# A decoder kernel whose constants and loads of x become pieces of the planned block

## The chip, the cores and the metric

The kernel runs on 1 core of a Trainium2 chip. The metric is the device time of one execution in microseconds. The chip has five engines with queues of their own: TensorE (PE, matrix products; PEld is its loading of weights), VectorE (DVE), ScalarE (ACT), GpSimd (POOL) and SyncE (SP, which here issues nearly all DMAs). Engines wait for each other through semaphores.

## The reference, cut to what matters

Two decoder layers over x, 2 sequences of 1024 rows of 256 numbers. Layer 0 is causal self attention, cross attention over 77 context rows and a mixture of 8 linear experts. Layer 1 has a recurrence over the 1024 positions in the place of self attention, then cross attention and a gated mixture of 16 experts beside a shared one.

```python
x = x + _L0_attn_ref(_layernorm(x, axis=-1), L0_attn_w_qkv, L0_attn_w_proj)
x = x + _L0_xattn_ref(_layernorm(x, axis=-1), ctx_768, mask_BxS2_bf1, L0_xattn_Wq, L0_xattn_Wk, L0_xattn_Wv, L0_xattn_Wo)
x = x + _L0_ffn_ref(_layernorm(x, axis=-1), L0_ffn_Wg, L0_ffn_bg, L0_ffn_We, L0_ffn_be)
x = x + _L1_attn_ref(_layernorm(x, axis=-1), L1_attn_Wi, L1_attn_bi, L1_attn_Wh, L1_attn_bh)
x = x + _L1_xattn_ref(_layernorm(x, axis=-1), ctx_768, L1_xattn_wq, ..., L1_xattn_bo)
x = x + _L1_ffn_ref(_layernorm(x, axis=-1), L1_ffn_router_w, ..., L1_ffn_shared_down_w)
```

The recurrence (`_L1_attn_ref`) is h(t) = tanh(Wi x(t) + bi + Wh h(t-1) + bh). Step t needs step t-1, so its 1024 steps run one after the other.

## The kernel before, in words

The rows are cut into 4 chunks of 512 (256 of each sequence, 4 tiles of 128). Every operation of every layer and chunk is a *piece*: a small function that waits on semaphores and issues a few instructions. A stage's pieces are all put into one block. `st.add(engine, name, function, count, cost, rank, after, ...)` registers a kind of piece: its engine, how many there are, an assumed cost in us, a rank (the lower one goes first) and how long after its end its signal is assumed to be seen. `Plan.make` then walks through time with these assumed numbers. At each turn it takes, over all engines, the piece that could begin earliest, and among equals the one of lowest rank; a piece can begin once the semaphores that it waits for are reached, which `Rehearsal` finds out by running the piece's function on a recorder. The outcome is a fixed order of pieces on each engine. So a shift of a few tenths of a microsecond at the start can change which piece goes first at any later place.

Between two steps of the recurrence the planner fits other pieces where it expects room. Where it expects PE to pause for over 0.1 us it puts in idle matmuls (L536, class `Recurrence`), whose result nobody reads.

The names that matter below:

- `tanh` (L562, L563) and `sub` (L568) with the products L519: the recurrence's step on ACT, DVE and PE.
- `ChunkNorm`: statistics (L435, L437, L440, DVE), `power` (L446, POOL, reads `neg_half`), `normalise` (L453, DVE), `turn` (L460, PE, transposes with `ident`); it serves all six layer norms.
- L764 with L776 and L787: queries and keys of the self attention of a chunk, rounded, and kept in two parts; they go to the DRAM tensors `q_scr`, `k_scr` and come back into `heads` by DMA.
- L968/L971 and L977: scores, mask (`mask_qk`, `identb`) and their row maxima; L1026/L1029 scores the other way round (`mask_kq`); L1040 the exponential; L1055 the product with the values.
- L749, L1251, L1263, L1294, L1305, L1319: the same for cross attention; `x_qs` is loaded by DMA from `qx_scr`.
- L1459/L1485: the experts of layer 0. L1687/L1755: gate and up, and down products of layer 1's gated experts, the last work of a chunk; `cT` (L1658) and `spread` (L1716, reads `sel_pair`) belong to it.
- `fill` (L2067, L2070): memsets of `heads`, 10 large ones before the first scores.
- `load` (L1925 to L1942): the loads of ctx, mask and weights of layer 0.

Before all that, `constants` runs a block of its own: SP issues the 8 loads of x and the one of wqkv, DVE sets eight constants, POOL waits for all eight and shapes seven of them, and the block's end is a barrier for all engines. The planned block comes behind it, and the planner is told by `given` that x and wqkv are there at time 1.0.

## Time and profile before

| | |
|---|---|
| median of 3 runs | 1354.29 us (1351.82 to 1355.94) |
| the profiled execution's own time | 1351.89 us |
| its span in the profile | 1350.2 us |
| mean granted clock of TensorE | 0.97 of full speed |
| PE busy | 1291.7 us, 96% |
| DVE busy | 857.6 us, 64% |
| ACT busy | 628.5 us, 47% |
| POOL busy | 38.7 us, 3% |

Busy shares are means over stages with different limits, and PE's includes the idle matmuls. A view by stretches of time and the waits in each tell more than the page's first lines.

### The profile page before, as it was taken

The numbers are of one execution on the slowest core, as the hardware profiler recorded it, in microseconds if no ns is written. First come the engines' busy times: TensorE is split into PE (matmuls) and PEld (weight loads), VectorE is DVE, ScalarE is ACT, GpSimd is POOL, SyncE is SP. The second block draws the span as 40 slices with busy tenths as digits, with TensorE's granted clock in tenths as the row PEclk, the third lists the DMA queues.
The fourth block names the chain that finished last, engine by engine and source line by source line (L and its number), as shares of the span: only waits on it lengthen the run. The fifth ranks groups of instructions, "written<-read, shape, count | busy, mean of one in ns | idle before, by whom it ended". The sixth has DMA issues, their size and how long they took to land.

```text
span 1350.2 us, 48630 instructions
## 1 busy us (share of the span) xinstructions
PE 1291.7 (96%) x19707; PEld 897.4 (66%) x19707; DVE 857.6 (64%) x2733; ACT 628.5 (47%) x2842; POOL 38.7 (3%) x60
## 2 busy tenths in 40 slices
PE   4598899999999999999999999999999999999998
PEld 2464446777766777776677777776767677766555
DVE  5875398258688326877762255677656575567586
ACT  2162403753533784443457865633544345442422
POOL 1010000000000000000000000000000000000000
PEclk9798779999999999999999998999999799999999
DMA  5536300001000000100000014010000100001000
GB/s 167 133 99 164 83 1 3 15 15 50 3 3 2 15 9 20 60 6 3 3 3 27 3 45 147 5 50 3 2 3 18 42 11 3 2 18 48 2 17 16
DMA packets 50753, 44.48 MB, mean 33 GB/s; under 512 B 10667, under 2 KB 49766, under 8 KB 50534
## 3 DMA queue, kind: packets, MB, share of 16 engines
q1 hardware_dynamic: 48934, 40.59, 10.2%
q8 instruction: 160, 2.62, 0.8%
q10 hardware_dynamic: 1600, 0.79, 0.3%
q14 instruction: 59, 0.48, 0.1%
HBM read 25.81 MB, written 15.15 MB: 30 GB/s over the span
## 4 chain that ended last, share of the span: by engine, by line
PE 90%; DVE 5%; DMA 2%; issue 1%; ACT 1%; SPq 1%; DVEq 0%; ACTq 0%
PE b L519 23%; PE b L1687 10%; PE b L1459 6%; PE b L536 6%; PE b L1055 6%; PE b L1026 5%; PE b L1755 5%; PE b L968 4%; PE b L701 3%; PE b L749 3%; PE b L1319 3%; PE b L1294 2%; PE b L63 2%; PE b L653 2%; DVE mx L977 2%; PE b L460 2%
## 5 line engine op out<-in xcount | busy, mean ns | idle before, releaser
L519 PEld LDWEIGHTS b<-hp,whp 128*128 128x128 f16 x12276 | 474.3, 96 | 242.1 <-ACT hp L562 157.9
L519 PE MATMUL b<-hp,whp 128*128 128x2 f16 x12276 | 531.3, 165 | 3.5 <-DVE hp L568 2.2
L568 DVE TENSOR_TENSOR hp<-hist,hp 128x4 f16<-128x4 f32 x1023 | 164.0, 160 | 347.9 <-ACT hist L563 337.0
L562 ACT ACTIVATE hp<-b 128x4 f16<-128x4 f32 x1024 | 178.1, 174 | 429.6 <-PE b L519 419.2
L977 DVE TENSOR_REDUCE mx<-b 128x1 f32<-128x512 f32 (+3 forms) x304 | 191.5, 652 | 2.5 <-PE b L971 1.8
L1040 ACT ACTIVATE vp<-b 128x512 f32<-128x512 f32 x288 | 171.1, 602 | 23.4 <-PE b L1029 9.5
L563 ACT ACTIVATE hist<-b 128x4 f32<-128x4 f32 x1024 | 177.7, 174 | 0.0
L1687 PE MATMUL b<-vp,heads 128*128 128x512 f16 x576 | 162.9, 381 | 0.0
L536 PE MATMUL b<-whp 128*128 128x512 f16 (+7 forms) x487 | 125.9, 332 | 0.0
L968 PE MATMUL b<-heads 128*128 128x512 f16 (+3 forms) x384 | 111.7, 335 | 2.3 <-DVE mx L977 1.2
L1459 PE MATMUL b<-we,xT 128*128 128x512 f16 x384 | 109.9, 380 | 0.0
L1026 PE MATMUL b<-heads 128*128 128x256 f16 (+1 forms) x640 | 104.9, 261 | 0.2
L1055 PE MATMUL b<-vp 128*32 128x256 f32 (+1 forms) x1280 | 95.2, 370 | 0.0
L1305 ACT ACTIVATE x_pr<-b 77x512 f32<-77x512 f32 x128 | 72.3, 592 | 14.6 <-PE b L1294 12.2
L1755 PE MATMUL b<-vp,heads 128*128 128x256 f16 x576 | 77.4, 272 | 0.0
L1485 DVE SCALAR_TENSOR_TENSOR x<-b,wts,x 128x256 f32<-128x256 f32 x128 | 61.7, 482 | 14.0 <-PE b L1459 7.1
L446 POOL TENSOR_TENSOR rs<-ve,neg_half 128x2 f32<-128x2 f32 x48 | 34.4, 717 | 1237.4 <-DVE ve L440 1237.4
L1687 PEld LDWEIGHTS b<-vp,heads 128*128 128x128 f16 x576 | 48.9, 97 | 23.6
L1026 PEld LDWEIGHTS b<-heads 128*128 128x128 f16 x640 | 52.9, 96 | 13.3 <-DVE mx L977 3.8
L1755 PEld LDWEIGHTS b<-vp,heads 128*128 128x128 f16 x576 | 52.1, 97 | 9.7 <-DVE heads L1739 0.3
L1263 DVE TENSOR_REDUCE x_nm<-b 128x4 f32<-128x308 f32 x128 | 56.9, 472 | 1.9 <-PE b L1251 1.3
L971 PE MATMUL b<-mask_qk,identb 128*128 128x128 bf16 x256 | 50.0, 224 | 0.0
(234 smaller groups left out, 1591.2 us busy)
## 6 DMA issues: line engine op xcount, KB each, us to landing
x_qs<-qx_scr SPq DMA_DIRECT2D x64, 96.0 KB
qx_scr<-xq_pair SPq DMA_DIRECT2D x16, 256.0 KB, 2.1
heads<-q_scr SPq DMA_DIRECT2D x32, 96.0 KB
heads<-k_scr SPq DMA_DIRECT2D x12, 192.0 KB, 4.3
x<-in_x SPq DMA_DIRECT2D x8, 256.0 KB, 6.1
q_scr<-tail SPq DMA_DIRECT2D x8, 256.0 KB, 2.4
k_scr<-tail SPq DMA_DIRECT2D x8, 256.0 KB, 2.3
x_qs<-in_L_ffn_We SPq DMA_DIRECT2D x2, 1024.0 KB, 5.4
```

What stands on the lines that cost most here:

```text
L519: return pe.matmul(self.z(t)[:, m], self.w.whp[:, a, k, m * P:(m + 1) * P], self.g.hp16[:, (t - 1) % 2, part, k, :], start=False, stop=Tru ...
L536: pe.matmul(self.g.b7[:, 0:min(512, columns - at)], self.w.whp[:, 0, 0, 0:P], self.w.whp[:].rearrange("p a k n -> p (a k n)")[:, 0:min(512 ...
L562: act.activation(self.g.hp16[:, t % 2, 0], self.z(t), ACT.Tanh, scale=1 / LIFT).then_inc(self.s["hi_ready"], 1)
L563: act.activation(self.g.hist[:, :, :, t % (4 * HALF)], self.z(t), ACT.Tanh, scale=1 / LIFT).then_inc(self.s["full_ready"], 1)
L968: last = pe.matmul(o[:, at:at + P * n], self.qs[:, H // 2 * (h % 2) + h // 2, column(j):column(j) + P], self.ks[:, b, h // 2, P * first:P ...
L977: v.tensor_reduce(self.mx[:, column(j) // P, head:head + heads, int(first > 0)], self.st.bank("self_first", i)[:, 0:P * n * heads].rearran ...
L1026: last = pe.matmul(o[:, N * e:N * e + N], self.ks[:, b, h // 2, P * kb:P * kb + P], self.qs[:, H // 2 * (h % 2) + h // 2, QW * b + first:Q ...
L1040: act.activation(self.pr[:, n % 2, e0:e0 + heads, first:QW], self.st.bank("self_s", i)[:, 0:N * heads].rearrange("p (e n) -> p e n", e=hea ...
L1055: last = pe.matmul(o[QD * e:QD * e + QD, QW * b + first:QW * b + QW], self.va[:, b * (S // P) + kb, at:at + QD], self.pr[:, n % 2, e, firs ...
L1459: last = pe.matmul(o[:], x[:, k, column(j):column(j) + P], self.w.we[:, wt, k, D * e:D * e + 2 * D], start=at == 0, stop=at == self.PER - 1)
L1687: last = pe.matmul(o[:], wt[:, k, m * P:(m + 1) * P], x[:, k, :], start=at == 0, stop=at == 5)
L1755: last = pe.matmul(o[:, D * (p % 2):D * (p % 2) + D], self.hp[:, n % 3, h, P * p:P * p + P], wd[:, m, :], start=m == 0 and p % 2 == 0 and ...
```

## The change

The block of `constants` goes. Its loads, memsets and affine selects become pieces of the planned block (class `Constants`), so the planner orders them with all others. Each engine's first reader of a constant waits for the semaphore `zeroed` or `shaped`. The selects on POOL now wait for one more memset each, no longer for all eight; `neg_half` is set first. By its rank, the loads of ctx, mask and some weights come between those of x.

```diff
-def constants(g, a):
-    nc = g.nc
+def constants(g):
...
-    with nc.Block() as block:
-        @block.sync
-        def _(sp):
-            src = a["x"].rearrange("(t p) d -> p t d", p=P)
-            for c in range(NK):
-                for b in range(B):
-                    at = b * (S // P) + 2 * c
-                    sp.dma_start(g.x[:, at:at + 2, :], src[:, at:at + 2, :]).then_inc(g.x_in[c], 16)
-                if c == 0:
-                    sp.dma_start(wqkv, a["L0_attn_wqkvT"].rearrange("(k p) n -> p k n", p=P)).then_inc(g.wqkv_in, 16)
...
-        @block.gpsimd
-        def _(pool):
-            pool.wait_ge(zeroed, 8)
...
+NEG_HALF_SET = 1
+IDENT, MASK_QK, MASK_KQ, TIE8, TIE16, SEL_PAIR = 1, 3, 4, 5, 6, 8
+
+
+class Constants:
+
+
+    def __init__(self, st, a):
+        self.g, self.a = st.g, a
+        st.add("sp", "load_x", self.load_x, NK, 1.0, lambda c: (-4100, -3850, -3650, -3640)[c], after=5.5)
+        st.add("sp", "load_qkv", self.load_qkv, 1, 0.5, lambda _: -4050, after=6.0)
+        st.add("v", "zero", self.zero, 8, lambda i: (0.1, 0.1, 0.1, 0.1, 0.1, 0.1, 0.3, 0.5)[i], lambda i: -3000 + i)
+        st.add("pool", "shape", self.shape, 8, lambda i: 0.3 if i < 4 else 0.4 if i < 6 else 1.25, lambda i: -3000 + i)
+
+    def load_x(self, sp, c):
+        src = self.a["x"].rearrange("(t p) d -> p t d", p=P)
+        for b in range(B):
+            at = b * (S // P) + 2 * c
+            sp.dma_start(self.g.x[:, at:at + 2, :], src[:, at:at + 2, :]).then_inc(self.g.x_in[c], 16)
...
+    def shape(self, pool, i):
+
+        g = self.g
+        pool.wait_ge(g.zeroed, min(i + 2, 8))
...
-    def make(self, programs, trial, signalled):
-        reached = {name: [1.0] * count for name, count in signalled}
+    def make(self, programs, trial):
+        reached = {}
...
     def power(self, pool, h):
         t = both(h)
+        if h == 0:
+            pool.wait_ge(self.g.zeroed, NEG_HALF_SET)
...
     def turn(self, pe, i):
         o = self.st.take(pe, self.name, i)
+        if i == 0:
+            pe.wait_ge(self.g.shaped, IDENT)
...
-    st.given(g.x_in, 32)
-    st.given([g.wqkv_in], 16)
+    Constants(st, a)
```

`load`, which is not edited, has ranks -3900, -3800, -3700 and so on, and so falls between `load_x` 0 and 1 and behind it.

**SP's queue at the very start of the program** (`x` are the loads of x, two for each chunk, `first` is wqkv, `vp` the context and the cross attention's Wk and Wv). Before:

```order
L89 DMA x<-in_x 128x2x256 x2
L91 DMA first<-in_L_attn_wqkvT 128x2x768
L89 DMA x<-in_x 128x2x256 x6
L82 UNCONDITIONAL_BRANCH
L385 UNCONDITIONAL_BRANCH
L1925 DMA mask<-in_mask 128x154
L1926 DMA vp<-in_ctxT 96x2x154
L1927 DMA vp<-in_L_xattn_Wk 96x2x256
L1928 DMA vp<-in_L_xattn_Wv 96x2x256
L1930 DMA wo<-in_L_attn_wo 128x2x256
```

And of the change:

```order
L100 DMA x<-in_x 128x2x256 x2
L104 DMA first<-in_L_attn_wqkvT 128x2x768
L1947 DMA mask<-in_mask 128x154
L1948 DMA vp<-in_ctxT 96x2x154
L1949 DMA vp<-in_L_xattn_Wk 96x2x256
L1950 DMA vp<-in_L_xattn_Wv 96x2x256
L100 DMA x<-in_x 128x2x256 x2
L1952 DMA wo<-in_L_attn_wo 128x2x256
L1954 DMA x_wq<-in_L_xattn_Wq 128x2x256
L1955 DMA x_wo<-in_L_xattn_wo 128x2x256
L100 DMA x<-in_x 128x2x256 x4
```

The two branches (end of the first block, start of the second) are gone, the context's loads come ahead of six of the eight loads of x, and the last four of x are behind the weights.

**DVE ahead of the first scores** (L453, in the change L464, is the second chunk's normalise; `heads`, `x_ks`, `x_vc` are memsets; L787, in the change L800, the rounding of queries and keys). Before:

```order
L787 SCALAR_TENSOR_TENSOR tail<-b,tail 128x512
L1121 MEMSET x_ks 128x1232
L1128 MEMSET x_vc 128x574
L2070 MEMSET heads 128x8x128
L1213 COPY x_vc<-b 77x16x16 x2
L2070 MEMSET heads 128x8x128 x5
L453 TENSOR_SCALAR first<-x,mv,rs 128x256 x4
L2137 TENSOR_TENSOR first<-b,first 128x2x128 x2
```

And of the change:

```order
L464 TENSOR_SCALAR first<-x,mv,rs 128x256 x2
L800 SCALAR_TENSOR_TENSOR tail<-b,tail 128x512
L464 TENSOR_SCALAR first<-x,mv,rs 128x256 x2
L800 SCALAR_TENSOR_TENSOR tail<-b,tail 128x512
L1138 MEMSET x_ks 128x1232
L1145 MEMSET x_vc 128x574
L2092 MEMSET heads 128x8x128
L1230 COPY x_vc<-b 77x16x16
L2092 MEMSET heads 128x8x128 x2
L1230 COPY x_vc<-b 77x16x16
L2092 MEMSET heads 128x8x128 x3
L2159 TENSOR_TENSOR first<-b,first 128x2x128 x4
```

The normalise of the second chunk has moved from behind these memsets to ahead of them.

**PE behind the recurrence's last step** (L519, in the change L532, is the step's product; L536 and L549 are idle matmuls, L460 and L473 transposes of a norm, L749 and L762 the last chunk's cross queries). Before:

```order
L519 MATMUL b<-hp,whp 128x2 x12
L536 MATMUL b<-whp 128x512 x5
L536 MATMUL b<-whp 128x128
L600 MATMUL b<-ident,hist 128x128 x2
L536 MATMUL b<-whp 128x512 x3
L536 MATMUL b<-whp 128x256
L600 MATMUL b<-ident,hist 128x128 x2
L536 MATMUL b<-whp 128x512 x18
L460 MATMUL b<-ident,n_xn 128x128 x2
L536 MATMUL b<-whp 128x512 x5
L460 MATMUL b<-ident,n_xn 128x128 x2
L749 MATMUL b<-xT,first 128x256 x8
```

And of the change:

```order
L613 MATMUL b<-ident,hist 128x128 x2
L1778 MATMUL b<-vp,heads 128x256 x3
L613 MATMUL b<-ident,hist 128x128 x2
L1778 MATMUL b<-vp,heads 128x256 x6
L1708 MATMUL b<-vp,heads 128x512 x12
L1739 MATMUL b<-mp,sel_pair 128x512
L1778 MATMUL b<-vp,heads 128x256 x12
L473 MATMUL b<-ident,n_xn 128x128 x2
L1778 MATMUL b<-vp,heads 128x256 x3
L1708 MATMUL b<-vp,heads 128x512 x5
L473 MATMUL b<-ident,n_xn 128x128 x2
L762 MATMUL b<-xT,first 128x256 x8
```

Gated experts' products (L1708, L1778) now stand where idle matmuls stood; in the whole program 47 of the former and 48 of the latter have moved from behind the last step to ahead of it, and further back in this part idle matmuls stand where the gated products stood.

## Rows read from the trace of the kernel before

**Rows 1.** The page, TensorE: busy us, share, instructions.

```profile
PE 1291.7 (96%) x19707; PEld 897.4 (66%) x19707; DVE 857.6 (64%) x2733; ACT 628.5 (47%) x2842; POOL 38.7 (3%) x60
```

**Rows 2.** Windows: stretch and length, busy us by engine, PEclk, DMA share, GB/s.

```profile
0.00:52.00 52.00, 20.51 (x100) 13.74 (x101) 34.96 (x94) 11.15 (x25) 7.13 (x16) 0.84 0.62 169
52.00:105.00 53.00, 48.73 (x503) 32.18 (x502) 44.55 (x114) 26.67 (x56) 4.26 (x6) 1.00 0.32 95
105.00:130.00 25.00, 22.01 (x118) 11.92 (x116) 13.35 (x29) 8.12 (x17) 0.00 (x0) 0.94 0.59 175
130.00:162.00 32.00, 25.34 (x155) 12.42 (x155) 10.31 (x25) 12.02 (x24) 0.00 (x0) 0.68 0.55 111
162.00:183.00 21.00, 16.79 (x98) 9.60 (x99) 20.10 (x59) 3.27 (x9) 1.48 (x2) 0.72 0.00 1
...
204.00:1214.00 1010.00, 1005.82 (x17761) 726.82 (x17761) 625.19 (x2183) 523.17 (x2633) 22.93 (x32) 0.99 0.06 20
1214.00:1350.00 136.00, 131.51 (x874) 79.56 (x872) 91.90 (x194) 42.73 (x77) 2.17 (x3) 1.00 0.06 21
```

**Rows 3.** The line of the first tanh, and ACT's timeline over one bare step.

```profile
L562 ACT ACTIVATE hp<-b x1024: 147/174/257, 204.3 to 1213.6; 128x4 f16<-128x4 f32 x171
...
1040.16 0.17 ACT L562 ACTIVATE hp<-b 128x4 f16<-128x4 f32 x1
...
1040.94 0.17 ACT L562 ACTIVATE hp<-b 128x4 f16<-128x4 f32 x1 [0.54 <-PE b L519]
```

**Rows 4.** Timeline of the start: start us, length, instruction, [idle before, releaser].

```profile
2.44 0.29 POOL L103 TENSOR_SCALAR_AFFINE_SELECT ident<-ident 128x128 f32<-128x128 f32 x1 [1.93 <-DVEq L82]
...
4.16 2.48 POOL L116 TENSOR_SCALAR_AFFINE_SELECT sel_pair<-sel_pair 128x1024 f16<-128x1024 f16 x2
...
7.92 0.17 DVE L2099 MEMSET bias<- 128x128 uint32 x1 [5.72 <-PEq L82]
...
8.74 0.36 DVE L435 BATCH_NORM_STATS2 bn<-x 128x6 f32<-128x256 f32 x1
...
13.85 0.73 DVE L453 TENSOR_SCALAR first<-x,mv,rs 128x256 f32<-128x256 f32 x2
...
16.68 2.42 PE L63 MATMUL b<-vp 96*128 96x154 f32 x8 [1.68 <-DMA vp<-in_L_xattn_Wv]
...
23.00 5.34 PE L764 MATMUL b<-first,x_pr 128*128 128x512 f16 x24
```

**Rows 5.** Timeline around the second chunk's normalise.

```profile
45.34 0.55 DVE L453 TENSOR_SCALAR first<-x,mv,rs 128x256 f32<-128x256 f32 x2
...
45.71 1.09 PE L460 MATMUL b<-ident,first 128*128 128x128 f32 x4 [14.99 <-DVE first L453]
...
53.06 4.28 DVE L977 TENSOR_REDUCE mx<-b 128x4 f32<-128x512 f32 x7 [1.59 <-PE b L971]
```

**Rows 6.** DVE's groups from 0 to 204 us: busy us, mean ns.

```profile
L977 DVE TENSOR_REDUCE mx<-b 128x2 f32<-128x512 f32 (+3 forms) x50 | 29.8, 631 | 1.6 <-PE b L971 1.6
```

**Rows 7.** The chain that ended last: start us, us, what.

```profile
9.25 7.39 DMA vp<-in_L_xattn_Wv
...
1226.47 2.59 PE b L1687 x12
```

**Rows 8.** Timeline of the tail, on PE, SP and DVE.

```profile
1221.11 3.62 PE L749 MATMUL b<-xT,first 128*128 128x256 f32 x16
...
1239.09 0.43 PE L1251 MATMUL b<-first,x_qs 128*128 128x154 f16 x4
...
1235.38 0.87 SPq L1235 DMA_DIRECT2D x_qs<-qx_scr  x2
...
1277.54 0.41 DVE L453 TENSOR_SCALAR n_xn<-x,mv,rs 128x256 f32<-128x256 f32 x1
...
1286.85 0.38 PE L460 MATMUL b<-ident,n_xn 128*128 128x128 f32 x2
...
1291.85 0.41 PE L460 MATMUL b<-ident,n_xn 128*128 128x128 f32 x2
```

More of the change, by code:

```diff
@@ L77, in constants @@
     g.sel_pair = g.sb("sel_pair", [P, MH - MS, P], F16)
[L78 removed]
+    g.zeroed, g.shaped = g.sem("zeroed"), g.sem("shaped")
     g.first = g.sb("first", [P, 3072])
[L80 removed]
     g.x_in, g.wqkv_in = [g.sem(f"x_in{c}") for c in range(NK)], g.sem("wqkv_in")
[L82 to L120 removed]
@@ L353, in __init__ @@
         self.ops = {e: {} for e in SEEN}
-        self.signalled = []
     def sb(self, name, shape, dt=F32):
@@ L364, in add @@
         self.plan.add(engine, name, count, cost, rank, after, **more)
-    def given(self, sems, count):
-        self.signalled += [(sem.name, count) for sem in sems]
     def bank(self, *key):
@@ L381, in run @@
         trial = {e: Rehearsal() for e in SEEN}
-        self.plan.make(self.ops, trial, self.signalled)
+        self.plan.make(self.ops, trial)
         order, ops = self.plan.order, self.ops
@@ L963, in first_pass @@
         pe.wait_ge(self.s["k_in"], 16 * 2 * B * (c + 1))
+        if i == 0:
+            pe.wait_ge(self.g.shaped, MASK_QK)
         for e in range(heads):
@@ L1021, in scores @@
         pe.wait_ge(self.m_in[hg % 2], 32 * ((c * NG + hg) // 2 + 1))
+        if i == 0:
+            pe.wait_ge(self.g.shaped, MASK_KQ)
         N = QW - first
@@ L1383, in route @@
             v.wait_ge(self.w.s["wg_split"], 3)
+        if i == 4:
+            v.wait_ge(self.g.shaped, TIE8)
         if step == 13 and c:
@@ L1585, in route @@
             v.wait_ge(*self.w.gated_in)
+        if i == 9:
+            v.wait_ge(self.g.shaped, TIE16)
         if step == self.STEPS - 1 and c:
@@ L1715, in spread @@
         pe.wait_ge(self.s["cpl"], 2 * c + 2)
+        if i == 0:
+            pe.wait_ge(self.g.shaped, SEL_PAIR)
         pe.matmul(o[:], self.g.sel_pair[:, m - MS, :], self.cps[:], start=True, stop=True
@@ L2243, in decoder @@
         g.qx_scr, g.kx_scr = (nc.dram_tensor(n, (D, PART, width), F16) for n, width in (("qx_scr", 2 * B * S), ("kx_scr", B * M2)))
-        constants(g, a)
+        constants(g)
         all_layers(g, a, out)
```

52 lines of the change are left out of this document (28 added, 24 removed).

## The prediction

> **What bounds the kernel now.** I read the page first: TensorE (PE) is busy 96% of the span, VectorE (DVE) 64% [rows 1]. A share that high does not say that PE is the limit, since the program fills gaps with idle matmuls (L536). So I cut the span where the recurrence starts and ends. Its first tanh (L562) starts at 204.3 us and its last at 1213.6 [rows 3]. That makes three parts: a head of 204.3 us before the first step, 1009.3 us of recurrence, and a tail of 136.6 us [rows 2].
>
> In the head no engine is full all the way. In the first 52 us PE works 20.5 us and DVE 35.0 us, and the clock's mean there is 0.84 [rows 2]. DVE stands still for 5.72 us until the first block's end lets it go, and its first statistics (L435) start at 8.74 us without waiting for x [rows 4]. PE's first long piece waits for the cross attention's Wv until 16.68 us, and the queries' products (L764) start at 23.00 us [rows 4]. Then PE waits 14.99 us for the second chunk's normalise (L453, 45.34 us), which stands on DVE behind eight memsets of `heads`, and the first reduction of maxima (L977) comes at 53.06 us [rows 5]. From 52 to 105 us DVE is busy 44.6 of 53 us, and from 162 to 183 us 20.1 of 21 us. Between these, from 105 to 162 us, DVE is half idle and PE runs part of the time at 1.2 GHz (mean clock 0.94 and 0.68) [rows 2].
>
> A step of the recurrence in which nothing is in the way takes 0.783 us [rows 3]; 1023 of them would take 801 us. They take 1009.3 us, so other work that PE does between the steps costs 208 us. I priced that work by columns, 512 columns of f16 at 2.59/12 = 0.216 us [rows 7] and fp32 at four times that (eight fp32 query products of 256 columns take 3.62 us, 0.45 each [rows 8]) (the 32-wide fp32 products L1055 and L1319 at a quarter of it), over the program's list: 631 us beside the steps, 127 us ahead of them and 131 us behind. In the tail 131 us of priced work stand against 136.6 us, and PE is busy 131.5 us: the tail is PE's own list, one after the other [rows 2].
>
> **The change part by part.** All engines' work is the same but for the moved constants, the two branches of the removed block, and 31 fewer idle matmuls. What changes is what overlaps, because the planner runs anew from time zero and every later place shifts. Read at the same places of both programs:
>
> *Start.* The eight memsets and the affine selects stay as they are; the barrier at their end goes, and the 5.72 us of DVE with it [rows 4]. The ctx loads are issued as numbers 4 to 7 of SP's queue, not behind all of x and the barrier. With the 7.39 us that Wv took [rows 7] and an issue near 3.9 us, it lands near 11.3 us. Its eight products (2.4 us), the first transposes and the stores then lead to L764 near 17 us, 6 us earlier. DVE's normalise of the first chunk hardly moves (13.85 us): it stays behind the split of wqkv, whose load is issued as before. The waits that the edit adds at first readers cost nothing: the constants needed first (`ident`, `neg_half`) are ready before 7 us, as POOL's last select ends at 6.64 us [rows 4], and the readers start after 12 us. If that cover went, it would be at most the 4.2 us that the selects take. SP's queue gains no work; x of chunks 2 and 3 now stands behind wo and the query weights, and its first reader is far later than 18 us.
> For the first L977 two bounds follow. Low: the barrier's 5.72 us less 2.5 us of work that now stands ahead of it on DVE (four more statistics and one more L787, against one memset of 1.76 us less; six short memsets only come earlier) is 3.2 us. High: DVE's whole idle time in the first 52 us, 17.0 us less 0.9 before its first instruction, less 2.5, is 13.6 us. I take 7 us, since the second chunk's normalise now stands ahead of seven memsets and no longer lets PE wait for them [rows 5], but the chain through L764, the stores to `q_scr`/`k_scr` and their loads moves only with the 6 us above.
>
> *Rest of the head.* Here 8.7 us more of PE's priced work and 16 more L977 (0.631 us each [rows 6], 10.1 us) stand ahead of the first step: self attention of the second chunk, pulled forward. In the DVE-full stretch after 52 us the list is 1.4 us shorter. Between L1251 and L1294, 2.7 us more of PE work stand in the way; I charge 2. Of the extra L977, eight lie beside the half-idle DVE of 105 to 162 us, free; two stand in the full stretch of 162 to 183 us, 1.3 us. Sum of the head: -7 - 1 + 2 + 1 = -5 us. Bounds: -13, and +4 if the gain at the start is the low one and the 2.7 and 1.3 us plus 3.5 us more at half clock are all paid.
>
> *Recurrence.* At the same step number all layer work now stands 20 to 38 steps earlier. So 47 of L1687 (10.2 us) and 48 of L1755 (5.2 us), with 1.5 us of their transposes and spreads, move from the tail in between the steps, 8.7 us of attention leaves to the head, and idle matmuls lose 1.5 us: +6.7 us. Averaged, a microsecond beside the steps costs 208/631 = 0.33 us; one in a step that is already over its room costs 1. The mean step is 0.2 us over the bare one, so most steps are full, and I take 0.75: +5 us. Bounds: +2 from the average price, +12 from the full price and 5 us for stalls at other places.
>
> *Tail.* The list is 18.3 us shorter, 1.4 us of it idle matmuls. Can the chain behind it follow? Until the first L1251 (1239.09 us) it can't, and need not: the lists are as long (14.4 us after the query products before, 13.9 now) [rows 8], as SP issues the last `x_qs` load at 1235.38 us. From there to the last L1319 the list is some 4 us shorter, of which I count 2. Behind it lies the large piece: the first row of the last chunk is normalised at 1277.54 us, but its transposes (L460) wait on PE behind some 60 gated matmuls until 1286.85 us, and the last comes at 1291.85 us [rows 8]. That is over 9 us of pure queueing; now those gated matmuls stand earlier and only idle matmuls lie between. The list from the last L1319 to 1292 us loses 15 us. From 1292 us to the end both lists are the same. I take -17 us in all; bounds -10 (the queueing alone) and -19.
>
> *Sum.* -5 + 5 - 17 = -17 us. Against the profiled execution (1351.9 us, 1.7 us around its span) that is 1334.9 us. It lies 2.4 us under the median of the runs, 1354.29 us, so I predict 1337 us.
>
> **The rivals.**
> *A. The recurrence gives it back.* The head starts the steps earlier, but pieces that fell in room now fall on full steps, and waits for other engines fall at new places. If the steps grow by 14 us, the sum is -5 + 14 - 17 = -8, 1346 us. For it: 0.2 us over the bare step on average. Against it: only 6.7 us are added to 631. Chance 0.17.
> *B. Nothing comes through* (the edit doesn't shorten the chain). The head's extra 8.7 us of PE work eat the start's gain (0), the tail's chain through the x_qs loads takes the place of PE and gives 6 us back, the recurrence costs its 7: about -4, 1350 us. Against it: the 9 us of queueing at 1277 to 1287 us. Chance 0.1.
> *C. Slower: the clock of the head.* From 130 to 183 us the mean clock was 0.68 and 0.72 with PE busy 80% [rows 2]. If it stays at 1.2 GHz from 130 us to the first step, the head's 57 us of priced work in that stretch take 114 us, not 74: +40 at the start, 1377 us; the forecast turns to slower once this costs more than 21 us. For it: 5.5 us more PE work stand there. Against it: that same work fills the pauses. Chance 0.06, with 0.03 for any other slower way.
> *D. Two engines on one port.* Before, POOL's selects (2.44 to 6.64 us) ran while DVE stood still [rows 4]; now DVE's memsets run beside them. If each blocks the other, DVE's first normalise comes up to 4.2 us later, and the first L977 gains 3 instead of 7 us: 1341 us. No row of before has the two side by side. Chance 0.14.
> The Trainium skill, "SBUF — State Buffer", section "SBUF: two separate sides", says that VectorE and GpSimd share one port pair as an exclusive lock in some modes, and that the loser waits for the whole instruction; by that rule D holds and the time is D's.
>
> On the clock: over the first 52 us, which hold PE's 15 us pause, its mean was 0.84, and from 52 to 105 us, with PE busy 48.7 of 53 us, it was full [rows 2]. The Trainium skill, "TensorE: Matmul & The Clock Gate", section "What's actually happening", says the same of pause and work; by that rule the fuller list of 130 to 183 us would hold 2.4 GHz, and the head would be shorter still: up to 6 us, 1331 us. My sum takes no part of it.
>
> **How the numbers follow.** The forecast (within 1328 to 1344 us by itself) has 0.5. A 0.17, B 0.1, C and other slower ways 0.09, D 0.14. A measurement tells a change from none at about 0.3%, 4 us: faster is under 1350.2 us. Faster: 0.5 + 0.14 + 0.15 of A + 0.02 of B = 0.81. Same: 0.02 of A + 0.08 of B = 0.10; slower 0.09. The range leaves out 0.2: 1324 us (head at -13, tail at -19) to 1352 us.
>
> **What would show it.** Right: the first tanh near 199 us; L764 near 17 us; no DVE idle time before 6 us; the first L977 near 46 us; 1010 to 1018 us between the first and last tanh; 119 us from the last tanh to the end, with the last L460 some 62 us after it. Wrong: a first tanh after 205 us, PEclk under 0.6 from 130 us on, a mean step over 1.0 us, or PE pauses of microseconds among L1251 and L1294 behind the last step.

## The result and the profile after

The changed kernel takes 1334.81 us (median of 4 runs, 1328.57 to 1341.89), the kernel before 1355.12 us beside it (4 runs, 1351.82 to 1357.02): a ratio of 0.987, 95% interval 0.9833 to 0.9907. In a later comparison, on one chip with 23 runs of the kernel before, it took 1336.51 us against 1350.86: 0.9891, interval 0.9843 to 0.9938.

The profiled execution took 1334.48 us. Its busy times, from the page:

```profile
PE 1290.1 (97%) x19676; PEld 891.6 (67%) x19676; DVE 858.2 (64%) x2733; ACT 624.9 (47%) x2842; POOL 38.4 (3%) x60
```

Against [rows 1] no engine does other work, but for TensorE's 31 matmuls less. The windows are cut where those of [rows 2] are, but for the ends of the recurrence (columns as there):

```profile
0.00:52.00 52.00, 31.16 (x145) 17.72 (x146) 40.39 (x108) 12.90 (x27) 8.70 (x18) 0.84 0.67 182
52.00:105.00 53.00, 47.83 (x476) 31.81 (x477) 42.88 (x107) 26.09 (x54) 2.75 (x4) 0.97 0.37 99
...
130.00:162.00 32.00, 28.38 (x218) 15.09 (x220) 22.93 (x60) 15.89 (x32) 1.39 (x2) 0.99 0.45 96
162.00:183.00 21.00, 19.07 (x159) 9.02 (x152) 18.86 (x48) 4.78 (x9) 0.00 (x0) 1.00 0.01 2
...
196.00:1214.00 1018.00, 1015.02 (x17735) 728.86 (x17733) 631.48 (x2191) 520.56 (x2631) 22.47 (x32) 0.98 0.06 19
1214.00:1333.00 119.00, 114.01 (x763) 68.91 (x761) 76.79 (x166) 36.00 (x69) 2.43 (x3) 1.00 0.07 23
```

The first 52 us hold 10.6 us more of TensorE's work than before. From 130 to 183 us the granted clock is 0.99 and 1.00, where it was 0.68 and 0.72, and VectorE does twice the work from 130 to 162 us (22.93 against 10.31 us). The line of the first tanh (L575 is the former L562) gives the three parts:

```profile
L575 ACT ACTIVATE hp<-b x1024: 146/173/262, 196.1 to 1214.0; 128x4 f16<-128x4 f32 x171
```

The head went from 204.3 to 196.1 us (-8.2, predicted -5), the recurrence from 1009.3 to 1017.9 (+8.6, predicted +5), the tail from 136.6 to 118.7 (-17.9, predicted -17).

The timeline of the start, where [rows 4] had VectorE idle for 5.72 us (L118 to L132 are the selects, L110 the memsets, L444 the statistics, L464 the normalise, L777 the query and key products):

```profile
1.33 0.29 POOL L118 TENSOR_SCALAR_AFFINE_SELECT ident<-ident 128x128 f32<-128x128 f32 x1 [0.82 <-DVE mask_kq L110]
...
3.05 1.16 POOL L132 TENSOR_SCALAR_AFFINE_SELECT sel_pair<-sel_pair 128x1024 f16<-128x1024 f16 x1
...
4.42 1.17 POOL L132 TENSOR_SCALAR_AFFINE_SELECT sel_pair<-sel_pair 128x1024 f16<-128x1024 f16 x1 [0.21 <-POOL sel_pair L132]
5.04 1.76 DVE L2089 MEMSET heads<- 128x2048 f32 x1 [0.38 <-issue]
6.74 0.36 DVE L444 BATCH_NORM_STATS2 bn<-x 128x6 f32<-128x256 f32 x1
...
11.10 0.73 DVE L464 TENSOR_SCALAR first<-x,mv,rs 128x256 f32<-128x256 f32 x2
11.15 2.42 PE L63 MATMUL b<-vp 96*128 96x154 f32 x8 [11.15 <-DMA vp<-in_L_xattn_Wv]
...
18.25 5.34 PE L777 MATMUL b<-first,x_pr 128*128 128x512 f16 x24
...
27.25 0.74 DVE L464 TENSOR_SCALAR first<-x,mv,rs 128x256 f32<-128x256 f32 x2
...
42.15 6.09 PE L777 MATMUL b<-first,x_pr 128*128 128x512 f16 x20
...
48.73 0.69 DVE L992 TENSOR_REDUCE mx<-b 128x4 f32<-128x512 f32 x1 [0.81 <-PE b L986]
```

VectorE's longest pause between its first memset and 5 us is 0.38 us. Wv lands at 11.15 us, the second chunk's normalise comes at 27.25 instead of 45.34 us [rows 5], and the first reduction of maxima at 48.73, 4.3 us earlier (predicted: 7). The selects and memsets lie side by side at the lengths that they had apart: 0.29 us for a 128x128 select, 1.16 and 1.17 for the two that together took 2.48, 1.76 for the long memset.

The tail behind cross attention, on TensorE and VectorE, against [rows 8] (L549 idle matmuls, L473 the router's transposes, L63 here its products):

```profile
1269.59 1.54 PE L549 MATMUL b<-whp 128*128 128x512 f16 x7
1270.15 0.40 DVE L464 TENSOR_SCALAR n_xn<-x,mv,rs 128x256 f32<-128x256 f32 x1
1270.96 0.38 PE L473 MATMUL b<-ident,n_xn 128*128 128x128 f32 x2
...
1274.34 0.41 PE L473 MATMUL b<-ident,n_xn 128*128 128x128 f32 x2
1274.59 0.60 PE L63 MATMUL b<-first,vp 128*128 128x16 f16 x18
```

The normalise is followed by its transposes 0.8 us later, not 9.3, and the last transposes come 60.3 us behind the last tanh instead of 78.3.

### The profile page after: what moved, and what is told of

Its sections match the earlier page's. It is cut to its first block, busy times and chain, and to the rows that moved or that the text cites. A ratio compares the mean times of both kernels' runs of the same rounds, so it can differ in the third digit from the quotient of the medians.

```text
span 1332.7 us, 48565 instructions
## 1 busy us (share of the span) xinstructions
PE 1290.1 (97%) x19676; PEld 891.6 (67%) x19676; DVE 858.2 (64%) x2733; ACT 624.9 (47%) x2842; POOL 38.4 (3%) x60
## 4 chain that ended last, share of the span: by engine, by line
PE 92%; DVE 4%; DMA 2%; issue 1%; ACT 1%; SPq 0%; DVEq 0%; ACTq 0%
PE b L532 24%; PE b L1708 10%; PE b L1478 7%; PE b L1072 6%; PE b L549 6%; PE b L1043 5%; PE b L1778 5%; PE b L983 5%; PE b L714 3%; PE b L762 3%; PE b L1336 3%; PE b L1311 2%; PE b L63 2%; PE b L473 2%; PE b L666 2%; PE b L518 2%
## 5 line engine op out<-in xcount | busy, mean ns | idle before, releaser
L532 PEld LDWEIGHTS b<-hp,whp 128*128 128x128 f16 x12276 | 477.6, 96 | 252.3 <-ACT hp L575 164.3
L532 PE MATMUL b<-hp,whp 128*128 128x2 f16 x12276 | 535.4, 165 | 2.7 <-DVE hp L581 1.6
L575 ACT ACTIVATE hp<-b 128x4 f16<-128x4 f32 x1024 | 178.2, 174 | 442.9 <-PE b L532 432.4
L1057 ACT ACTIVATE vp<-b 128x512 f32<-128x512 f32 x288 | 170.7, 603 | 33.1 <-PE b L1046 19.7
L1708 PE MATMUL b<-vp,heads 128*128 128x512 f16 x576 | 168.5, 385 | 0.0
L549 PE MATMUL b<-whp 128*128 128x512 f16 (+6 forms) x456 | 120.9, 335 | 0.0
L1778 PE MATMUL b<-vp,heads 128*128 128x256 f16 x576 | 78.2, 272 | 0.0
L457 POOL TENSOR_TENSOR rs<-ve,neg_half 128x2 f32<-128x2 f32 x48 | 34.2, 712 | 1232.3 <-DVE ve L449 1232.1
L1043 PEld LDWEIGHTS b<-heads 128*128 128x128 f16 x640 | 53.5, 96 | 14.3 <-DVE mx L992 4.4
L1708 PEld LDWEIGHTS b<-vp,heads 128*128 128x128 f16 x576 | 48.2, 97 | 20.1 <-DVE x_nm L1280 0.4
L1778 PEld LDWEIGHTS b<-vp,heads 128*128 128x128 f16 x576 | 51.5, 97 | 9.9 <-DVE heads L1762 0.6
L983 PEld LDWEIGHTS b<-heads 128*128 128x128 f16 x384 | 36.7, 98 | 24.0 <-DVE mx L992 12.2
```

What stands on the lines that cost most here:

```text
L532: return pe.matmul(self.z(t)[:, m], self.w.whp[:, a, k, m * P:(m + 1) * P], self.g.hp16[:, (t - 1) % 2, part, k, :], start=False, stop=Tru ...
L549: pe.matmul(self.g.b7[:, 0:min(512, columns - at)], self.w.whp[:, 0, 0, 0:P], self.w.whp[:].rearrange("p a k n -> p (a k n)")[:, 0:min(512 ...
L575: act.activation(self.g.hp16[:, t % 2, 0], self.z(t), ACT.Tanh, scale=1 / LIFT).then_inc(self.s["hi_ready"], 1)
L983: last = pe.matmul(o[:, at:at + P * n], self.qs[:, H // 2 * (h % 2) + h // 2, column(j):column(j) + P], self.ks[:, b, h // 2, P * first:P ...
L1043: last = pe.matmul(o[:, N * e:N * e + N], self.ks[:, b, h // 2, P * kb:P * kb + P], self.qs[:, H // 2 * (h % 2) + h // 2, QW * b + first:Q ...
L1057: act.activation(self.pr[:, n % 2, e0:e0 + heads, first:QW], self.st.bank("self_s", i)[:, 0:N * heads].rearrange("p (e n) -> p e n", e=hea ...
```

## The experiments

Twelve runs. Where a recurrence length stands with a *clock loss*, that is the sum over windows of 1 us of (1 - PEclk) between the first and the last tanh: what the stretches at 1.2 GHz add at most. "Cross stretch" is the first chunk's cross attention, from its first L1294 to the last reciprocal (L663, the eighth).

**Order, block and loads taken apart.** Three kernels, compared together with the kernel before (1351.16 us).

The changed code with the old order pinned, no block:

```diff
+        own = ("load_x", "load_qkv", "zero", "shape")
+        self.plan.kinds = [k for k in self.plan.kinds if k.name not in own]
...
         self.plan.make(self.ops, trial)
+        order["sp"] = [("load_x", 0), ("load_qkv", 0), ("load_x", 1), ("load_x", 2), ("load_x", 3)] + order["sp"]
+        order["v"] = [("zero", i) for i in range(8)] + order["v"]
+        order["pool"] = [("shape", i) for i in range(8)] + order["pool"]
```

> The order of all layer work is that of before, and so is the order of the loads; only the block of its own with its barrier is gone, the constants stand at the head of the planned block's queues. Theory 1 (the early start carries through): DVE's 5.72 us at the barrier come back, the first tanh stands at 199 us, not 204, and the whole takes about 1349 us. Theory 2 (the order does it): the start's gain is used up by waits on loads and on PE before the cross attention, the first tanh stays at 203 to 205 us and the time is that of before within 2 us.

1345.27 us, ratio 0.997 (0.9937 to 1.0002). Its timeline:

```profile
4.20 0.43 DVE L451 BATCH_NORM_STATS2 bn<-x 128x6 f32<-128x256 f32 x1 [1.05 <-DMA x<-in_x]
...
10.38 1.97 DVE L2180 SCALAR_TENSOR_TENSOR x_pr<-first,x_pr 128x384 f16<-128x384 f32 x4 [5.54 <-ACT x_pr L2175]
...
17.49 2.42 PE L63 MATMUL b<-vp 96*128 96x154 f32 x8 [2.00 <-DMA vp<-in_L_xattn_Wv]
```

The statistics start 4.5 us earlier, but VectorE then waits 5.54 us for the split of wqkv, and Wv still lands at 17.5 us. The first L977 comes at 52.76 us, 0.3 us earlier than before, and the first tanh at 204.3 us, as the second theory has it: in the old order the barrier is worth next to nothing. The median lies 5.9 us under that of the kernel before beside it, more than that theory allows, but the interval includes no change, and this profile has a clock loss of only 3.4 us in its recurrence, where the profile of before has 12.

The new order, but constants and x in the old block with its barrier:

```diff
+        with self.nc.Block() as block:
+            @block.sync
+            def _(sp):
+                for name, i in [("load_x", 0), ("load_qkv", 0), ("load_x", 1), ("load_x", 2), ("load_x", 3)]:
+                    ops["sp"][name](sp, i)
...
+                pool.wait_ge(self.g.shaped, 8)
+        order = {e: [x for x in order[e] if x[0] not in own] for e in order}
```

> The order of all layer work is that of the change, but the loads of x and wqkv and the constants stand in a block of their own with its barrier ahead of it, as before. Theory 1: without the early start the first tanh comes 5 us or more later than in the change (201 to 204 us), 1340 to 1343 us in all. Theory 2: the first tanh stays under 200 us, since the stretch of the cross attention is as short as in the change, and the tail is 118 to 120 us: 1335 to 1339 us in all.

1341.91 us, ratio 0.9926 (0.9887 to 0.9964). Head 202.0, recurrence 1011.8, tail 118.6 us: the tail's whole gain comes with the order. The head came out as the first theory says, and the time too. Its first L977 (L1011 there), its first L1294 (L1330), its line of the first tanh, and the window of its cross stretch beside that of the changed kernel:

```profile
54.66 0.69 DVE L1011 TENSOR_REDUCE mx<-b 128x4 f32<-128x512 f32 x1 [0.59 <-PE b L1005]
...
141.34 0.80 PE L1330 MATMUL b<-x_qs,x_ks 128*77 128x256 f16 x4
...
L594 ACT ACTIVATE hp<-b x1024: 147/174/257, 202.0 to 1213.7; 128x4 f16<-128x4 f32 x171
...
141.30:156.30 15.00, 14.69 (x131) 7.05 (x131) 7.66 (x18) 10.94 (x21) 0.00 (x0) 1.00 0.58 123
...
135.50:150.40 14.90, 14.67 (x131) 7.03 (x131) 7.56 (x18) 10.93 (x21) 0.00 (x0) 1.00 0.55 124
```

Both kernels have the same order and a cross stretch of 14.9 us at full clock, and they differ by the block and the order of the loads alone. The changed kernel is 5.9 us ahead at L977 (48.73), 5.9 at L1294 (135.5) and 5.9 at the first tanh (196.1). So in the new order the early start is worth 5.9 us, and all of it reaches the first step.

The first of these kernels (old order of the layers' work, no block) with the new order of loads: ctx and Wv ahead of six of the eight loads of x:

```diff
+        order["sp"] = [("load_x", 0), ("load_qkv", 0), ("load", 0), ("load_x", 1), ("load", 1), ("load", 2),
+                       ("load_x", 2), ("load_x", 3)] + order["sp"][3:]
```

> As the first of these kernels, and the loads of the context come ahead of six of the eight loads of x, as in the change. Theory 1: Wv lands near 11 us, the queries' products start 4 us earlier and the first tanh comes at 197 to 199 us, 1347 us in all. Theory 2: DVE's order ahead of the second chunk's normalise is the old one, so PE still waits for it; the first L977 comes at most 2 us earlier than in the kernel without the load order, and the first tanh stays at 202 to 205 us.

1351.77 us, ratio 0.9993 (0.9959 to 1.0028). L764 comes at 21.23 us, the first L977 2.9 us earlier than before (2.6 earlier than without the new loads), the first tanh at 202.1 us; tail 136.6. The time can't be told from no change either. The median lies 6.5 us above that of the first of these kernels, though the first tanh comes 2.2 us earlier: medians of these kernels don't resolve such differences, and the head is better read from the profiles.

**The cross stretch of the head.** In the kernel before it takes 28.9 us, in the changed one 14.9. Two causes were visible, the clock of 0.68 and a stall on ScalarE. The kernel before with idle matmuls in the pauses:

```diff
+            if name == "x_first" and i < 16: pe.append(("warm", 384))
+            if (name, i) == ("x_scores", 3): pe.append(("warm", 12 * 512))
+            if name == "self_v" and i in (14, 15): pe.append(("warm", 3 * 512))
```

> The kernel before, with idle matmuls added on PE in the first chunk's cross attention: 384 columns behind each L1251 pair, 6144 where PE waits 5 us for DVE's L787, and twice 1536 behind. The clock theory (PE at 1.2 GHz from 127 to 154 us is what made the stretch long): L1294 and L1319 keep their length at full clock, the stretch from the first L1294 to the last reciprocal (L663, 160.3 us) shrinks from 28.9 to 21 to 23 us, and the first tanh comes 5 to 8 us earlier. The stall theory (ACT waited 8.3 us for the q_scr store, and PE behind it): the wait stays as it is, the stretch shrinks by at most 3 us, 1352 us in all.

1340.21 us, ratio 0.9926 (0.9891 to 0.9961): faster than before, by work that computes nothing. The window 130:162 has the full clock:

```profile
130.00:162.00 32.00, 27.44 (x202) 15.47 (x201) 15.21 (x40) 13.13 (x27) 0.69 (x1) 1.00 0.54 112
```

The cross stretch takes 23.2 us (-5.7), the first tanh comes at 197.7. How much -5.7 is worth shows the profile of a later kernel (the one with thinned matmuls) whose head is untouched: at a mean clock of 0.68 its stretch took 25.9 us, 3 us less than that of before.

The stall in the kernel before, on ScalarE's timeline and on SP's:

```profile
128.63 0.60 ACT L776 ACTIVATE tail<-b 128x512 f16<-128x512 f32 x1 [0.48 <-DMA q_scr<-tail]
137.54 0.60 ACT L776 ACTIVATE tail<-b 128x512 f16<-128x512 f32 x1 [8.31 <-DMA q_scr<-tail]
...
142.51 2.05 ACT L1305 ACTIVATE x_pr<-b 77x512 f32<-77x512 f32 x4 [1.71 <-PE b L63]
...
126.46 2.93 SPq L1284 DMA_DIRECT2D x_qs<-x_mp  x4
129.56 1.87 SPq L949 DMA_DIRECT2D heads<-k_scr  x4
131.47 2.88 SPq L1284 DMA_DIRECT2D x_qs<-x_mp  x4
134.40 0.44 SPq L810 DMA_DIRECT2D q_scr<-tail  x1
```

ScalarE waits for a staging buffer whose store SP issues behind twelve others, and the exponentials (L1305) stand behind that wait in its order. The store moved up:

```diff
+        sp[at:at + 6] = [("qk_keep", 13), ("x_load_max", 2), ("x_load_max", 3),
+                         ("qk_keep", 14), ("self_load_k", 1), ("qk_keep", 15)]
```

> The kernel before with six entries of SP's list in another order: the store of q and k piece 13 goes ahead of self_load_k 1 and x_load_max 2 and 3, and self_load_k 1 behind the store of piece 14. Theory stall: in the kernel before the first chunk's cross attention (first L1294 to the eighth L663, 28.9 us) loses time because ScalarE stands 8.3 us for the staging buffer that this store must empty, with the exponentials x_pr behind it in its order, and TensorE behind those; then this reorder alone makes the stretch 3 to 6 us shorter, the first tanh 3 to 6 us earlier than 204.3 us, and ScalarE's wait for q_scr under 4 us. Theory clock alone: the stretch is long because TensorE runs at 1.2 GHz in it; then the reorder changes it by less than 1.5 us. The recurrence and the tail stay.

1346.91 us, ratio 0.9965 (0.9928 to 1.0001). The same two waits of ScalarE, and the window:

```profile
133.57 0.60 ACT L781 ACTIVATE tail<-b 128x512 f16<-128x512 f32 x1 [3.97 <-DMA q_scr<-tail]
...
137.28 2.05 ACT L1310 ACTIVATE x_pr<-b 77x512 f32<-77x512 f32 x4 [1.08 <-PE b L63]
...
130.00:162.00 32.00, 27.34 (x205) 15.60 (x205) 19.78 (x51) 14.36 (x31) 1.48 (x2) 0.93 0.52 112
```

The exponentials start 5.2 us earlier, the cross stretch falls to 18.8 us and the first tanh to 194.4. That is 10 us, more than expected, and the clock rose with it, from 0.68 to 0.93: the stall left TensorE idle for 5.1 us from 133.8 us, and within that pause the clock fell for the second time, from 137 to 154 us. With the store moved up the pause is 0.9 us, and this second fall is gone.

Then the idle matmuls and the reordered store in one kernel, by the two diffs above:

> Both edits, the reordered store and the idle matmuls that held the clock in the first chunk's cross attention. The idle matmuls alone took the stretch from the first L1294 to the eighth L663 from 28.9 to 23.2 us; the changed kernel has 14.9 us. If stall and clock are the two causes and add up, it falls to 17 to 20 us, the first tanh comes at 193 to 196 us, ahead of the changed kernel's 196.1, and the whole takes about 9 to 11 us less than the kernel before. If they are the same microseconds seen twice, it stays at 22 to 24 us.

1333.83 us (4 runs, 1332.38 to 1340.16), ratio 0.9889 (0.9853 to 0.9925). The cross stretch takes 19.8 us, the first tanh stands at 193.8. So the two overlap: at full clock the reordered store is worth 3.4 us (23.2 to 19.8), at 0.68 the idle matmuls 5.7, and both together 9 to 10. The median is 19.7 us under that of the kernel before beside it, the ratio stands for 15 us (10 to 20), and 9 to 11 were expected. This profile has no stretch at half clock in its recurrence, which takes 1000.2 us, 9 less than in the profile of before; whether the edit has a part in that, no run tells.

**The queueing in the tail.** The prediction took 9 us of the tail's gain from transposes that wait behind some 60 gated matmuls. The kernel before with these and the 12 behind them made thin (24 of L1687 and 48 of L1755; the rest of their columns is left out):

```diff
+        n = 64 if 408 <= i < 432 else 512
+        last = pe.matmul(o[:, 0:n], wt[:, k, m * P:(m + 1) * P], x[:, k, 0:n], start=at == 0, stop=at == 5)
...
+            to = 32 if 124 <= i < 140 else D
```

> The kernel before, with the gated matmuls that stand on TensorE between the last output projection of cross attention (L701) and the first transposes of the router (L460, 1286.85 us) made narrow: 24 gate/up pieces on 64 of 512 columns, 16 down pieces on 32 of 256. It leaves out the rest of their columns, some 12 us of matmuls. If these only queue in front of the transposes, the normalise at 1277.54 us stays where it is relative to the last tanh and the part from the last tanh to the end shrinks from 136.6 us by 9 to 11 us, to 126 to 128 us; the further 8 us of the change's tail then come from the gated matmuls ahead of it, between the last tanh and L701. If another wait takes the place of PE there (the normalise's own chain, the accumulation of a down piece, the experts' selection), the tail shrinks by less than 5 us. Head and recurrence as before, 204 and 1003 to 1010 us.

1353.1 us, ratio 1.0001 (0.9964 to 1.0038). From the last tanh to the end it is 137.2 us: nothing gained. VectorE's and TensorE's timeline of the thinned kernel there, and a window:

```profile
1282.28 0.69 DVE L1740 TENSOR_TENSOR heads<-tail,heads 128x512 f16<-128x512 f32 x1 [0.69 <-ACT heads L1736]
1282.89 0.41 DVE L453 TENSOR_SCALAR n_xn<-x,mv,rs 128x256 f32<-128x256 f32 x1
...
1283.03 2.74 PE L1757 MATMUL b<-vp,heads 128*128 128x256 f16 x12 [2.14 <-DVE heads L1740]
...
1285.99 3.75 PE L536 MATMUL b<-whp 128*128 128x512 f16 x10
...
1278.00:1292.00 14.00, 10.37 (x78) 6.08 (x79) 7.43 (x17) 3.17 (x7) 0.00 (x0) 0.63 0.12 39
```

VectorE's list has the elementwise work of the gated blocks (L1701 to L1740) ahead of the second normalise of the router, which comes at 1282.89 us, 71.2 us behind the last tanh where it was 73.8. The first transposes do come earlier, at 68.5 instead of 73.3 us behind the last tanh. But the last come at 78.9 instead of 78.3, for the clock fell to half in the new pauses: twelve down matmuls of full width took 2.74 us there and 1.48 before, ten idle ones 3.75 and 2.29. So this run mixes two things, and from the lengths of these two groups I estimate that at full clock it would have gained nearly 3 us (1.26 + 1.46). VectorE's side was then thinned too, alone and with TensorE's:

```diff
+    def width(self, n):
+        return 64 if 31 <= n < 36 else 512
...
+        w = self.width(i)
+        t = self.th[:, i % 3, 0:w]
```

Six functions take their columns from this width: tanh, silu, product, weigh, keep_hidden and hidden_low.

> The kernel before with the elementwise work of gated blocks 31 to 35 (tanh, silu, product, weighing and splitting of the hidden units, on ScalarE and VectorE) on 64 of 512 columns; TensorE's matmuls are all there. It leaves the other columns of these blocks out. If VectorE alone held the router's transposes back once TensorE was thinned, but TensorE's queue is as long, nothing moves: the tail stays within 2 us of 136.6 us. If VectorE's list is what binds and TensorE only stands in its shade, the tail falls by 6 us or more.

> Thinned matmuls (24 gate/up pieces, 16 down pieces) and thinned elementwise work together, in the kernel before; the other columns are left out. Thinning the matmuls alone moved the first router product by no more than 0.3 us against the last tanh. Two queues side by side: with both short the tail falls by 8 to 12 us, from 136.6 to 125 to 129 us. If something else holds it (the clock, which fell to 0.63 when TensorE had pauses there, or the chain from L703 through normalise and transposes), by less than 5 us.

The elementwise work alone: 1348.5 us, ratio 1.0005 (0.9966 to 1.0043), and 136.3 us from the last tanh to the end. Both: 1345.16 us, ratio 0.9964 (0.9933 to 0.9996), and 128.7 us: 7.9 less, just under what was expected of two queues side by side. The transposes in the last:

```profile
1274.87 0.42 PE L460 MATMUL b<-ident,n_xn 128*128 128x128 f32 x2
...
1280.71 0.60 PE L63 MATMUL b<-first,vp 128*128 128x16 f16 x18
```

From the last L1319 to the first router product it is 28.3 us before, 20.6 with both thinned and 13.1 in the changed kernel.

**The price of a microsecond between the steps.** The kernel before with 197 idle matmuls of 512 columns:

```diff
+            if name == "lo" and i % 5 == 0 and 20 <= i <= 1000:
+                pe.append(("idle", 512))
```

> The kernel before with 512 more idle columns on TensorE behind the low part of every fifth step from 20 to 1000, 197 of them, 42.6 us by 0.216 us each. It prices a microsecond put in between the steps. The prediction took 0.75 for the moved gated matmuls: 32 us longer from first to last tanh (1035 to 1042 us). At the average price of 0.33 it would be 14 us (1017 to 1024); at full price 43 us (1045 to 1052). Head and tail as before, 204 and 136.6 us.

1382.73 us, ratio 1.0242 (1.0214 to 1.027). Its line of the first tanh:

```profile
L568 ACT ACTIVATE hp<-b x1024: 147/174/257, 205.9 to 1242.4; 128x4 f16<-128x4 f32 x171
```

The recurrence takes 1036.5 us, with a clock loss of 1.7: 1034.8 without it. The nine profiles with the old order and no filling lie at 996.3 to 1000.2 us without theirs, 998.0 on average. 36.8 us for 42.6 us of matmuls: 0.86. To take off the whole clock loss is a little too much, though: the lengths of these nine (1000.2 to 1010.9 us) follow 999.9 us plus 0.76 us for each microsecond of clock loss, to within 1.2 us. By that line the filled kernel is 35.3 us longer, 0.83.

**The changed kernel again, and with its start warmed.**

First without an edit:

> The changed kernel once more, on the same chip and beside the same runs of the kernel before, with a second profile. Head 196 us and tail 118.7 us as in the first profile, since both follow the order. The recurrence took 1017.9 us with stretches at half clock that cost 15 us by the sum of (1 - granted clock) over 1 us slices; without them the new order has 1003 to 1005 us, the old one 996 to 1000. So this profile should have 1003 to 1005 us plus what its own half-clock slices sum to. If the recurrence's growth is the order's alone, it has 1017 to 1019 us whatever the clock.

The second profile has the first tanh at 202.1 us and the last at 1214.8, tail 118.7. Its clock:

```profile
28.00:45.00 17.00, 10.61 (x38) 5.55 (x39) 14.21 (x31) 3.35 (x9) 2.27 (x3) 0.60 0.84 192
130.00:162.00 32.00, 30.09 (x190) 15.97 (x189) 18.25 (x47) 12.65 (x25) 0.69 (x1) 0.76 0.38 89
```

So the head of the changed kernel is not 196 us but 196 to 202: this time TensorE ran at 0.76 from 130 to 162 us and the cross stretch took 20.2 us, with the same instructions. The expectation of a fixed head failed. Its recurrence is 1012.6 us with a clock loss of 8.5, 1004.1 without.

Then with idle matmuls in three pauses of the start:

```diff
+            if (name, i) == ("self_v", 3): pe.append(("warm", 5120))
+            if (name, i) == ("x_v", 0): pe.append(("warm", 2048))
+            if (name, i) == ("x_v", 1): pe.append(("warm", 8192))
```

> The changed kernel with idle matmuls (128 columns each, from two of the constants into the bank that idle matmuls use) in three pauses of TensorE: 5120 columns behind the first chunk's last self_v, 2048 behind x_v 0 and 8192 behind x_v 1. In the changed kernel the clock stood at 0.52 and 0.50 from 28 to 45 us, and 20 query and key products (L777) took 6.1 us there, where 24 took 5.3 us at full clock. If TensorE's own time leads to the first L992 (48.73 us), it comes 2 to 4 us earlier and the first tanh (196.1 us) 1 to 3 us earlier. If the DMA queues or VectorE lead there, or VectorE's full list behind it takes the gain as it took that of the start before, the first tanh moves by less than 1 us though the clock is full. Recurrence and tail as in the changed kernel, 1018 (less if the clock dips less) and 118.7 us.

1328.88 us (6 runs, 1326.65 to 1334.14), ratio 0.9855 (0.9818 to 0.9892). It is the fastest kernel of this study by its median, though its interval overlaps that of the changed kernel beside it. The window and the products (L794 is L777 there):

```profile
28.00:45.00 17.00, 12.97 (x125) 9.32 (x126) 15.07 (x33) 4.38 (x10) 2.27 (x3) 1.00 0.86 193
...
41.45 4.48 PE L794 MATMUL b<-first,x_pr 128*128 128x512 f16 x20
```

Twenty products take 4.48 us, not 6.09, and the first reduction of maxima comes at 46.42 us, 1.4 and 2.3 us before those of the two profiles without. The first tanh at 198.4 lies between theirs (196.1 and 202.1), and the cross stretch took 19.0 us at a clock of 0.73, so at the first step the gain isn't shown. The profiled execution was the slowest of the six, 1334.14 us.

## Why the prediction was right, and where it was not

The forecast was 1337 us, faster; 1334.81 was measured. The parts came as -8.2, +8.6 and -17.9 us for -5, +5 and -17. The sizes of the recurrence and the tail held. That of the head held by luck: all four of its terms were too favourable (-4.3, +2.9, +5.6 and +1.7 us for -7, -1, +2 and +1), and a stretch that the prediction doesn't price, cross attention's with -14.0 us, made up for them. The head in pieces, us:

| | before | changed | changed, again | new order, old block | forecast of the change |
|---|---|---|---|---|---|
| to the first L977 | 53.1 | 48.7 | 47.9 | 54.7 | -7 |
| on to the first query product of cross attention (L749) | 51.7 | 54.6 | 54.0 | 54.0 | -1 |
| on to the first L1294 | 26.5 | 32.2 | 33.3 | 32.7 | +2 |
| cross stretch | 28.9 | 14.9 | 20.2 | 14.9 | none |
| on to the first tanh | 44.0 | 45.7 | 46.9 | 45.7 | +1 |
| first tanh | 204.3 | 196.1 | 202.1 | 202.0 | -5 |

**Start (-7).** What it named came nearly as said: L777 at 18.25 us (predicted near 17), no idle VectorE before 5 us. The first reduction of maxima moved by 4.3 us, nearer to the low bound (3.2) than to the 7 I took. The early start itself gives 5.9 us there (48.73 against 54.66 in the new order with the old block), but the new order by itself takes 1.6 us (54.66 against 53.06). Another reason is in the profile of after: TensorE's 17 us from 28 us on ran at half clock, and warming them gave 1.4 to 2.3 us. That a gain at the start is handed on to the first step held: 5.9 us of 5.9 in the new order, 2.2 of 2.6 for the loads in the old one. What does not hold is that the barrier alone makes that gain; in the old order it gave 0.3 us. Two small readings were off as well: of the eight memsets ahead of the second chunk's normalise six are of `heads` and two of other tiles, and the first reader of `neg_half` (POOL, L457) ran at 8.19 us, not after 12 us, which cost nothing, as it had been set by 0.95 us.

**Rest of the head (+2).** By the first query product of cross attention (L762, 103.39 us against 104.89 of L749) 1.5 us of the start's gain were left: the stretch that I had down as 1 us shorter took 2.9 us more. Up to the first L1294 I charged 2 us, and it took 5.6 more, so that the first L1294 came 4.1 us later. That is the self attention pulled forward, and I priced it too low. What I left out is the cross stretch behind it, 28.9 us against 14.9 and 20.2. Two runs price its parts. At full clock the old order takes 23.2 us and the new 14.9, 8.3 less; 3.4 of it is the store that stood late in SP's queue, and for the other 4.9 I have no run. At a clock of 0.68 and 0.76 it is 28.9 and 20.2, 8.7 less (5.7 if the 25.9 us of the profile with the untouched head are taken). The clock itself moves either by some 5.5 us. So the planner's new order removed a stall that I had not looked for (SP issues its last store of queries and keys at 118.18 us, 17 us ahead of the first L1294, and ScalarE has no wait for `q_scr` behind it), since I priced the stretch by TensorE's columns and not by who waits for whom. It pays back what the pieces pulled forward cost.

The sum of the head, -5, came out near: five profiles with the old head have their first tanh at 200.8 to 205.9 us (203.8 on average), the two of the changed kernel at 196.1 and 202.1, 4.7 less on average. The two groups overlap, so the size is not firm.

**Recurrence (+5).** Without their clock losses the old order takes 998.0 us (nine profiles) and the new 1003.8 (four: 1002.6, 1005.0, 1003.4, 1004.1): +5.8. By the line of 0.76 us for each microsecond of loss the new order stands at 1006.3 us, +6.4. For 6.7 us of list that is 0.87 to 0.96, and the filled steps gave 0.83 to 0.86; I took 0.75. The rest of the measured +8.6 is half-clock stretches, of which the two profiles compared had 15.3 and 11.9 us. The same order had 0 to 13.7 us.

**Tail (-17).** It measured -17.9, the same in every profile of either order (136.6 us where nothing was thinned, and 118.6 to 118.7). The sizes of the pieces held too: -2.7 to the last L1319 (I counted 2), -15.2 from there to the router (15). But the step "that is over 9 us of pure queueing" was wrong as it stood. Thinning the matmuls gave nothing: VectorE had a list nearly as long in front of the same transposes, and half clock took back what was gained at the first of them. Thinning VectorE's side alone gave nothing either, and both 7.9 us. The change moves whole gated blocks into the recurrence, matmuls and elementwise work together, and so shortens both queues. What moving the matmuls alone would have given, no run shows. The other 7.5 us between 20.6 and 13.1 us are not taken apart by a run either.

**The rivals.** *A* (the recurrence gives it back, +14) and *B* (nothing comes through) are out by these numbers. *C*: the clock did not stay at 1.2 GHz from 130 to 183 us, but it is no constant: 0.99 and 1.00 in one profile of the changed kernel, 0.76 and 0.92 in the other. From 130 to 162 us the four profiles of the new order have 0.76 to 0.99, the seven of the old one whose head is as before or only started earlier 0.52 to 0.71. *D*: the rows of the start show selects and memsets side by side, none longer than apart, and the normalise came at 11.10, earlier than 13.85 us. The rule of the Trainium skill, "SBUF — State Buffer", section "SBUF: two separate sides", that VectorE and GpSimd lock each other out, does not show in these instructions. Its condition there is a VectorE instruction in a mode with two ports or with two inputs from SBUF, and a memset has no input; that the rule speaks for *D* was read into it. The remark on the clock, by the Trainium skill, "TensorE: Matmul & The Clock Gate", section "What's actually happening", that work holds the clock and pauses lose it, is borne out by the idle matmuls: 0.68 to 1.00 in that window, and 6.6 us off the first tanh. Whether the fuller list does the same is not shown apart: the old order with the store moved up has 0.93 there, without more work, so the pause that went may be enough.

## What to carry to other kernels

A piece that waits behind one engine's queue may wait behind a second of the same length: before pricing a queue at what it holds, read what the waiting instruction's own producer is doing, and thin both, alone and together. What an edit at the start wins depends on the order behind it, and must be followed to the stage that counts: here removing the barrier gave 0.3 us in the old order, removing it and moving the loads 5.9 us in the new one, and 5.9 us arrived at the first step. Test such an edit in both orders. Where TensorE has pauses of some microseconds ahead of work on the critical path, idle matmuls in them are a cheap thing to try: here about 0.7% of the time on one kernel.

## What the hardware showed beyond that

In the recurrence, with TensorE busy 98 to 100% of the whole, the granted clock drops to half for 3.4 to 13.7 us at a time, and single steps there take 1.4 to 2.4 us. The longest of the changed kernel:

```profile
1018.00:1032.00 14.00, 14.00 (x145) 9.52 (x145) 3.84 (x18) 3.54 (x24) 0.00 (x0) 0.51 0.13 45
```

The places are not random. In ten profiles of the old order and four of the new one, every such stretch begins at one of a few steps:

| order | steps at which the clock falls (profiles that have it) |
|---|---|
| old (10 profiles) | 178 (5), 619 (8), 697 or 698 (4), 856 or 857 (4) |
| new (4 profiles) | 164 to 166 (3), 589 or 590 (3), 712 to 715 (3), 819 (1), 971 to 973 (4) |

So the order of the work sets where the clock may fall, and which of these places an execution takes differs: one profile of the old order has none. At two of them, 619 in the old order and 589 in the new, TensorE has just paused for 1.2 to 2.2 us, because VectorE stands for the load of the down weights with the step's own L568 behind it in its list (a load that a kernel could issue earlier, which no run tries):

```profile
813.19 0.18 DVE L2053 TENSOR_SCALAR first<-first 128x32 f16<-128x32 f32 x1 [2.75 <-DMA heads<-in_down]
...
813.91 0.27 PE L519 MATMUL b<-hp,whp 128*128 128x2 f16 x4 [2.17 <-DVE hp L568]
```

In the one profile of the old order where this pause was 0.4 us the clock did not fall there, nor did it in one of the nine others. At the other places no pause of TensorE over 0.3 us lies in the 8 us ahead (ahead of 1018 us none over 0.15), so pauses are not the only thing after which the clock falls; the cause there stays open. Over the profiles the clock losses sum to 0 to 15 us in a recurrence of 1000 us, and to another 9 to 31 in the head. The spread between executions of one kernel is of that size (1341.59 to 1361.96 us over 23 runs). A difference of 5 us between two single profiles of this kernel means nothing before the clock has been taken out of it.
